# Softmax stage of a four-layer graph network: ScalarE's scaled copies split between its exponentials, two VectorE products back to back, and two of ten numerators on GpSimd

## The chip, the cores and the metric

The kernel runs as one program on one core of a Trainium2 chip. The metric is the device time of that core in microseconds (us), the median of several runs. A core has TensorE (PE in the profile; PEld is its weight load), VectorE (DVE), ScalarE (ACT), GpSimd (POOL) and SyncE (SP, which here only issues transfers). Each engine works through its own list of instructions in order and waits on semaphores, which other engines and transfers raise.

## What is computed

Four graph layers run over 6250 nodes with 16 features and 206250 edges sorted by target node: a double graph convolution, an attention layer with a softmax per edge and channel, a relational layer and an edge-network layer. The change lies in the attention layer (and one semaphore is renamed in the set-up). Cut to what matters, with 256 channels (16 x 16) for each edge:

```python
h_src = feat[src][:, :, None]
e1 = (efeat @ W_msg + b_msg).reshape(E, 16, 16) * h_src      # message
e2 = (efeat @ W_attn + b_attn).reshape(E, 16, 16) * h_src    # logit
seg_max = segment_max(e2, dst)
ex = exp(e2 - seg_max[dst])
denom = segment_sum(ex, dst)
ft = segment_sum(e1 * ex / denom[dst], dst).sum(axis=1)
```

## The kernel before

The edges are laid out as 125 partitions of 1650 edges. The softmax stage goes through them in NB1 = 165 **blocks** of B1 = 10 **steps**; a step is one edge in each partition, with 512 values in each: 256 logits and 256 messages, interleaved in groups of 16. Buffers come in threes (slot s = b % 3). All loops on the chip carry three blocks in a body; what follows is the work for block b, with the name that the text uses. GROUPS = (2, 2, 2) are the steps 0 to 5 (AT = 6), which VectorE multiplies by the gathered features; steps 6 to 9 (NA = 4) are done by ScalarE.

- **Gathers** (GpSimd, `gather`, L594): ten indirect transfers of feature rows, those of steps 6 to 9 first. They wait until ScalarE has done with the slot (`soft_ap`).
- **Edge products**: TensorE multiplies a step's edge features with the weights, into PSUM. `products` (L1094) does two steps at a time for VectorE, `scalable` (L1105) one step for ScalarE, into two banks in turn.
- **Feature products P0, P1, P2** (VectorE, `product`, L1747): two steps each, read from PSUM and multiplied by the gathered features, which is one operand in PSUM and one in the SBUF.
- **Scaled copies C6 to C9** (ScalarE, `scaled`, L808): one of the steps 6 to 9 as 16 small instructions of 32 columns, from PSUM into PB. C7, C8 and C9 of block b+1 and C6 of block b+2 are done while block b is worked on.
- **Maxima T0 to T18** (VectorE, `top`, L1736 and L1740): a running maximum forward over the ten steps and nine steps back. Each depends on the one before.
- **Differences D0 to D5** (TensorE, L1152 and L1153; D5, half as long, L1156 and L1157): logits minus maximum of two steps, with an identity and a negated identity as weights, in two PSUM banks in turn. D0 waits for T10, D1 for T12, D2 for T14, D3 for T16, D4 and D5 for T18. From D2 on, each also waits for the exponential that used its bank two before (`soft_exp`).
- **Exponentials E0 to E5** (ScalarE, L849, E5 at L852): one for each difference.
- **Numerators** (VectorE, `weigh`, L1757): message times exponential, for steps 0-1, 2-3, 4-5 (512 values a partition each) and 6-9 (1024 values), both operands in the SBUF.
- **Carry** (VectorE, L1766) and **first sum** (TensorE, `first_sum`, L1113 and L1115): the block before is joined on; the carry waits for E5 and the second half of the first sum waits for the carry.
- **Row sums R1 to R8** (VectorE, `row_sum`, L1779), the **last sum** (TensorE, `last_sum`, L1121 and L1122, after R8 and E4), and ScalarE's copies of the first and last row (`first_rows` L816, `last_rows` L827, with `last_keep` L820 between).
- **Stores** (SP, L365): maxima and two tables of sums. The second half of a block's sums waits for `last_rows`; P0 of the block three later waits until all of them have landed (`soft_s`).

VectorE's order is written out by hand (`soft` from L1813): while it takes the maxima of block b it does numerators, carry and row sums of block b-1. Before the change it reads: T0, P1, T1, T2, P2, T3, T4, numerators 0-1, T5, carry, T6, T7, R1, T8, numerators 2-3, T9, R2, T10, R3, T11, numerators 4-5, T12, R4, T13, numerators 6-9, T14, R5, T15, R6, T16, P0 of b+1, T17, R7, T18, R8. ScalarE's order in block b is: C7 of b+1, last_rows of b-2, last_keep, C8 of b+1, first_rows of b-1, C9 of b+1, E0, E1, E2, E3, C6 of b+2, E4, E5. TensorE's is: first sum of b-1, edge products of b+1 for C8, C9, P0 and P1, then D0 to D3, the edge products for C6 of b+2 and for P2, D4, D5, the last sum of b-1, the edge product for C7 of b+2.

Of the kernel before, what the change touches and what calls it, by code (L numbers as in the profile page):

```python
# [13 lines left out]
N, E, F = 6250, 206250, 16  # L14
P = 125
# [8 lines left out]
B1 = 10  # L24
NB1 = C // B1
# [3 lines left out]
AT = sum(GROUPS)  # L29
NA = B1 - AT  # L30
SUB = 33
SUBW = C // SUB
MAXES = 2 * B1 - 1
# [74 lines left out]
def graph_layers(nc, A, out):  # L108
# [5 lines left out]
    with ctx:  # L114
# [467 lines left out]
        def _(gp):  # L582
# [57 lines left out]
            narrow("conv2")  # L640

            gp.wait_ge(S("tab_feat"), 16 * (NT + 1))
            for b in range(NB1):
                s = b % 3
                if b >= 3:
                    gp.wait_ge(S("soft_ap"), NA * (b - 2))
                for t in range(AT, B1):
                    gather(GH[:, s, t, :], d_feat, srci[:, b * B1 + t:b * B1 + t + 1], f"soft_late_g{s}")
                for t in range(AT):
                    if b >= 3 and t % 2 == 0:  # L650
                        gp.wait_ge(S("soft_prod"), NG3 * (b - 3) + t // 2 + 1)
                    gather(GH[:, s, t, :], d_feat, srci[:, b * B1 + t:b * B1 + t + 1], f"soft_g{s}")
            for s in range(3):
                gp.wait_ge(S(f"soft_s{s}"), 160 * THIRD)
# [22 lines left out]
        def _(act):  # L677
# [119 lines left out]

            def scaled(b, s, k, t):

                n = t - AT  # L800
                act.wait_ge(S("soft_am"), NA * b + n + 1)
                if n == 0:
                    act.wait_ge(S(f"soft_late_g{s}"), 16 * NA * (k + 1))
                    if not isinstance(b, int) or b >= 3:
                        act.wait_ge(S("soft_num"), 4 * (b - 2))
                bank = (4 + n % 2) * 512
                for i in range(F):
                    ins = act.activation(PB[:, s, n, 2 * F * i:2 * F * (i + 1)], PS[0:P, bank + 2 * F * i:bank + 2 * F * (i + 1)],  # L808
                                         ACT.Copy, scale=GH[:, s, t, i:i + 1])
                ins.then_inc(S("soft_ap"), 1)  # L810

# [17 lines left out]
            def soft(b, s, k, first, left):  # L829
# [12 lines left out]
                for n in range(6):  # L842
                    if n == 4 and left >= 2:
                        scaled(b + 2, (s + 2) % 3, k + (s >= 1), AT)
                    act.wait_ge(S("soft_diff"), 6 * b + n + 1)
                    bank = PS[0:P, (6 + n % 2) * 512:(7 + n % 2) * 512]
                    if n < 5:
                        t = B1 - 2 - 2 * n
                        act.activation(paired(XD[:, s, t:t + 2, :], 0), bank.rearrange("p (x o) -> p x o", o=F), ACT.Exp)\  # L849
                           .then_inc(S("soft_exp"), 1)  # L850
                    else:
                        act.activation(DC, bank[:, 0:CH], ACT.Exp, bias=KR[:, s, 0, 0:1]).then_inc(S("soft_exp"), 1)  # L852

            act.wait_ge(S("h_soft"), 1)
# [52 lines left out]
        def _(pe):  # L907
# [29 lines left out]

            pe.wait_ge(S("diag"), 1)
            pe.matmul(PS[:, 3072:3072 + P], ones[0:P, :], diag[:, :], start=True, stop=True).then_inc(S("run_p"), 1)
# [168 lines left out]
            def first_sum(b, s):  # L1108

                pe.wait_ge(S("soft_exp"), 6 * b + 6)  # L1110
                pe.wait_ge(S("soft_num"), 4 * b + 1)
                bank = PS[0:P, 3584:4096]
# [12 lines left out]
            def soft(b, s, k, first, left):  # L1125
# [9 lines left out]
                for n in range(6):  # L1135
                    if n == 4 and left >= 2:
                        scalable(b + 2, (s + 2) % 3, k + (s >= 1), AT)
# [93 lines left out]
        def _(dve):  # L1231
# [118 lines left out]
            v.tensor_copy(small[0:R, 640:640 + F * F], PS[0:R, 2560:2560 + F * F]).then_inc(S("wrel"), 1)  # L1350
            v.tensor_scalar(diag[:, :], ident[0:P, 0:P], one_run[:, 0:1], None, ALU.mult).then_inc(S("diag"), 1)
            dve.wait_ge(S("run_p"), 1)
# [416 lines left out]
            def row_sum(b, s, t):  # L1769
# [5 lines left out]
                else:  # L1775
                    if t in (2, 4, 6):
                        dve.wait_ge(S("soft_num"), 4 * b + t // 2 + 1)
                    dve.wait_ge(S("soft_sum"), (B1 - 2) * b + t - 1)
# [9 lines left out]
            def late_sums(b, s):  # L1788

                weigh(b, s, 0, 2)  # L1790
                carry(b, s)
# [4 lines left out]
                weigh(b, s, 4, 2)  # L1796
                weigh(b, s, AT, NA)
                for t in range(4, B1 - 1):
# [14 lines left out]
            def soft(b, s, k, left):  # L1813
# [3 lines left out]
                top(b, s, 0)  # L1817
                product(b, s, 1)
                top(b, s, 1)
                top(b, s, 2)  # L1820
                product(b, s, 2)
                top(b, s, 3)
                top(b, s, 4)
                weigh(o, z, 0, 2)
                top(b, s, 5)
                carry(o, z)
                top(b, s, 6)
                top(b, s, 7)
                row_sum(o, z, 1)
                top(b, s, 8)  # L1830
                weigh(o, z, 2, 2)
                top(b, s, 9)
# [7 lines left out]
                top(b, s, 13)  # L1840
                weigh(o, z, AT, NA)
                top(b, s, 14)
                row_sum(o, z, 5)
                top(b, s, 15)
                row_sum(o, z, 6)
                top(b, s, 16)
# [123 lines left out]
```

## Time and profile before

| what | value |
|---|---|
| median of 3 runs | 9713.91 us (9710.63 to 9717.96) |
| the profiled execution's own time | 9719.54 us |
| its span in the trace | 9717.7 us |
| busy in the span: TensorE, VectorE, ScalarE, GpSimd | 80%, 75%, 31%, 71% |
| the softmax stage's first to last carry (L1766) | 3023.6 to 6394.8 us, 164 blocks of 20.56 us |

The stage is a third of the span. In it, VectorE is the busiest engine. The trace's rows give an instruction's start, its duration, the engine, the line in the kernel, the operation, what it writes and reads, the shape, how many instructions are merged in the row, and in square brackets the idle time before it with what ended that time. Durations of neighbours on an engine overlap a little, since the next instruction starts while the last one drains: the cost of an instruction in a full engine is the distance from its start to the next start. The "granted clock" is TensorE's clock as a share of 2.4 GHz; it has two levels, 2.4 and 1.2 GHz (0.5).

### The profile page before, as it was taken

The numbers are of one execution on the slowest core, as the hardware profiler recorded it, in microseconds if no ns is written. First come the engines' busy times: TensorE is split into PE (matmuls) and PEld (weight loads), VectorE is DVE, ScalarE is ACT, GpSimd is POOL, SyncE is SP. The second block draws the span as 40 slices with busy tenths as digits, with TensorE's granted clock in tenths as the row PEclk, the third lists the DMA queues.
The fourth block names the chain that finished last, engine by engine and source line by source line (L and its number), as shares of the span: only waits on it lengthen the run. The fifth ranks groups of instructions, "written<-read, shape, count | busy, mean of one in ns | idle before, by whom it ended". The sixth has DMA issues, their size and how long they took to land.

```text
span 9717.7 us, 129425 instructions
## 1 busy us (share of the span) xinstructions
PE 7811.0 (80%) x35487; PEld 4162.5 (43%) x35487; DVE 7305.6 (75%) x13006; ACT 3031.2 (31%) x12664; POOL 6877.6 (71%) x5177
## 2 busy tenths in 40 slices
PE   0799995999965888888888888845888985899994
PEld 0465553555532333333333333313555653455552
DVE  2566662555536999999999999986888885788884
ACT  0111111000005777777777777731000000000000
POOL 5688886788877766666666666636888886688887
PEclk6899996999987999999999999967999997899996
DMA  1344442233324777777777777765323231433332
GB/s 32 94 114 110 102 104 48 61 76 70 69 38 117 203 203 207 204 203 202 203 205 206 203 202 203 204 192 157 82 70 82 70 82 37 107 100 100 100 105 48
DMA packets 823092, 1218.47 MB, mean 125 GB/s; under 512 B 237316, under 2 KB 687320, under 8 KB 802209
## 3 DMA queue, kind: packets, MB, share of 16 engines
q1 hardware_dynamic: 574895, 999.46, 34.3%
q0 software_dynamic: 212624, 110.62, 9.8%
q10 hardware_dynamic: 35440, 106.85, 3.5%
q8 instruction: 55, 0.90, 0.0%
q14 instruction: 78, 0.64, 0.0%
HBM read 421.45 MB, written 788.86 MB: 125 GB/s over the span
## 4 chain that ended last, share of the span: by engine, by line
POOL 45%; PE 17%; ACT 16%; issue 13%; DVE 5%; DMA 2%; SPq 1%; DVEq 0%; ACTq 0%; POOLq 0%
POOL arena L594 45%; ACT arena L808 14%; PE PS L1152 5%; PE PS L1153 4%; PE PS L1121 2%; PE PS L985 2%; PE PS L1122 1%; ACT arena L849 1%; DVE arena L1912 1%; PE PS L1113 1%; PE PS L1115 1%; PE PS L1105 1%; ACT arena L827 1%; DVE arena L1736 1%; DMA arena<-d_lane 1%
## 5 line engine op out<-in xcount | busy, mean ns | idle before, releaser
L985 PE MATMUL PS<-arena,TB 128*128 128x500 bf16 (+1 forms) x16038 | 3546.8, 376 | 225.0 <-DVE TB L1650 179.3
L594 POOL DMA_INDIRECT arena<-d_feat,srci x1650 | 2127.3, 1289 | 1237.7 <-ACT arena L808 753.8
L985 PEld LDWEIGHTS PS<-arena,TB 128*128 128x128 bf16 x16038 | 1581.0, 100 | 1862.7 <-issue 217.7
L594 POOL DMA_INDIRECT arena<-d_h,srci x1485 | 1959.2, 1319 | 569.8 <-issue 451.1
L808 ACT ACTIVATE arena<-PS,arena 125x32 f32<-125x32 f32 x10560 | 2012.0, 445 | 354.9 <-PE PS L1105 323.8
L1435 DVE TENSOR_SCALAR arena<-arena,lane 128x2000 bf16<-128x2000 f16 (+2 forms) x1848 | 1228.6, 723 | 576.3 <-DMA arena<-d_lane 330.6
L594 POOL DMA_INDIRECT arena<-d_rel,irel x858 | 1208.7, 1409 | 313.0 <-issue 261.2
L594 POOL DMA_INDIRECT arena<-d_nn,srci x759 | 1069.2, 1409 | 295.0 <-issue 230.4
L1152 PE MATMUL PS<-arena,ident 125*125 125x512 f32 x1650 | 962.6, 666 | 312.1 <-DVE arena L1740 211.7
L1447 DVE SCALAR_TENSOR_TENSOR arena<-arena,lane,PS 128x500 f32<-128x500 f16 x891 | 632.2, 712 | 626.0 <-PE PS L988 534.3
L1153 PE MATMUL PS<-arena 125*125 125x512 f32 x1650 | 887.6, 621 | 0.0
L1779 DVE SCALAR_TENSOR_TENSOR arena<-arena 125x512 f32<-125x512 f32 x1155 | 856.7, 742 | 0.3
L1736 DVE SCALAR_TENSOR_TENSOR arena<-arena 125x256 f32<-125x256 f32 x1650 | 786.7, 477 | 31.7
L1467 DVE TENSOR_TENSOR_SCAN arena<-keep,arena 125x50 f32<-125x50 f32 x2640 | 586.0, 296 | 267.7 <-DMA arena<-d_h,srci 258.9
L1008 PEld LDWEIGHTS PS<-fold,arena 128*125 128x125 f32 x5214 | 688.2, 194 | 218.7 <-DVE arena L1447 93.0
L1008 PE MATMUL PS<-fold,arena 128*125 128x16 f32 (+1 forms) x5214 | 639.3, 255 | 120.4 <-ACT arena L718 107.3
L849 ACT ACTIVATE arena<-PS 125x512 f32<-125x512 f32 x825 | 566.5, 754 | 467.6 <-PE PS L1153 467.5
L1740 DVE SCALAR_TENSOR_TENSOR arena<-arena 125x256 f32<-125x256 f32 x1485 | 704.6, 474 | 0.4
L1747 DVE TENSOR_TENSOR arena<-PS,arena 125x1024 f32<-125x1024 f32 x495 | 601.1, 1214 | 39.6 <-DMA arena<-d_feat,srci 33.8
L1152 PEld LDWEIGHTS PS<-arena,ident 125*125 125x125 f32 x1650 | 273.3, 198 | 790.3 <-issue 465.2
L703 ACT ACTIVATE arena<-PS 125x432 f32<-125x432 f32 (+1 forms) x66 | 35.4, 537 | 1672.2 <-PE PS L1008 1672.2
L1757 DVE TENSOR_TENSOR arena<-arena 125x512 f32<-125x512 f32 (+1 forms) x660 | 544.7, 825 | 4.6 <-ACT arena L849 4.6
(285 smaller groups left out, 7692.9 us busy)
## 6 DMA issues: line engine op xcount, KB each, us to landing
d_smax<-arena SPq DMA_DIRECT2D x165, 1120.0 KB
d_sums_low<-arena SPq DMA_DIRECT2D x330, 560.0 KB
d_sums_high<-arena SPq DMA_DIRECT2D x330, 560.0 KB
arena<-d_pick SPq DMA_DIRECT2D x66, 843.8 KB
d_x<-arena ACTq DMA_DIRECT2D x165, 241.7 KB
arena<-d_x SPq DMA_DIRECT2D x165, 241.7 KB
arena<-d_lane SPq DMA_DIRECT2D x66, 527.3 KB
d_rel<-arena SPq DMA_DIRECT2D x50, 669.4 KB
```

The lines of the kernel that those rows point to most:

```text
L594: gp.indirect_dma_start(out=dst, out_offset=None, in_=table, in_offset=bass.IndirectOffsetOnAxis(ap=index, axis=0)).then_inc(S(sem), 16)
L808: ins = act.activation(PB[:, s, n, 2 * F * i:2 * F * (i + 1)], PS[0:P, bank + 2 * F * i:bank + 2 * F * (i + 1)], ACT.Copy, scale=GH[:, s, ...
L849: act.activation(paired(XD[:, s, t:t + 2, :], 0), bank.rearrange("p (x o) -> p x o", o=F), ACT.Exp)\
L985: pe.matmul(PS[:, acc_at(L, q):acc_at(L, q) + w], TB[:, part, g * LANES * F:(g + 1) * LANES * F], OH[L][i][:, g, at:at + w], start=g == 0 ...
L1008: ins = pe.matmul(PS[0:P, 3584 + t * w:3584 + (t + 1) * w], lanes, fold[:, 0:w], start=True, stop=True)
L1152: pe.matmul(bank.rearrange("p (x o) -> p x o", o=F), ident[0:P, 0:P], paired(pairs, 0), start=True, stop=False)
L1153: pe.matmul(bank, neg, XM[:, s, t:t + 2, :].rearrange("p t c -> p (t c)"), start=False, stop=True)\
L1435: ins = v.tensor_scalar(OH[L][i][:, c, 0:n], PI[L][s][:, at:at + n], lane[:, c:c + 1], None, ALU.is_equal)
L1447: v.scalar_tensor_tensor(MK[L][:, acc_slot(L, q), 0:n], LI[L][s][:, q * QW:q * QW + n], lane[:, NG:NG + 1], PS[:, acc_at(L, q):acc_at(L, q ...
L1736: v.scalar_tensor_tensor(wide_row(XM[:, s, n, :]), wide_row(prev), KR[:, s, n, 0:1], logits, ALU.add, ALU.max).then_inc(S("soft_max"), 1)
L1740: v.scalar_tensor_tensor(XM[:, s, t, :], XM[:, s, t + 1, :], KR[:, s, t + 1, 0:1], XM[:, s, t, :], ALU.add, ALU.max).then_inc(S("soft_max" ...
L1779: v.scalar_tensor_tensor(to, last, KR[:, s, t, 1:2], to, ALU.mult, ALU.add).then_inc(S("soft_sum"), 1)
```

## The change

- **ScalarE**: C6 of block b+2 is no longer one run of 16 copies between E3 and E4. Four of its copies follow each of E0, E1, E2 and E3. Its wait for the buffer is now for the numerators 6-7 of block b-1 on VectorE and for GpSimd's multiplication of that block, where it was for all four of VectorE's numerator instructions.
- **TensorE**: the edge product for C6 of block b+2 stands ahead of D0, where it stood ahead of D4. It waits until C8 of block b+1 is done, since it uses the same PSUM bank. The first sum waits for two numerator instructions instead of one.
- **VectorE**: P2 follows P1 directly. The numerator instruction for steps 6 to 9 becomes one for steps 6 and 7, and comes early. The new order is T0, P1, P2, T1, numerators 6-7, T2, T3, numerators 0-1, T4, carry, T5, numerators 2-3, T6, T7, R1, T8, T9, R2, T10, R3, T11, numerators 4-5, T12, R4, T13, R5, T14, R6, T15, T16, P0 of b+1, T17, R7, T18, R8.
- **GpSimd**: the numerators of steps 8 and 9 of block b-4 are one multiplication of 512 values a partition, after the third gather of block b, and it waits until T0 of block b-3 is done. R8 waits for it.
- The semaphore `diag` becomes the fourth count of `wa`; nothing else hangs on that.

```diff
--- before.py
+++ after.py
@@ -639,6 +639,16 @@
             gp.wait_ge(S("tab_conv2"), 16 * (NT + 1))
             narrow("conv2")
 
+            def last_numerators(b):
+
+                s = b % 3
+                gp.wait_ge(S("soft_exp"), 6 * b + 1)
+                if b < NB1 - 1:
+                    gp.wait_ge(S("soft_max"), MAXES * (b + 1) + 1)
+                rows = XD[:, s, B1 - 2:B1, :]
+                gp.tensor_tensor(paired(rows, 1), paired(PB[:, s, NA - 2:NA], 1), paired(rows, 0), ALU.mult)\
+                    .then_inc(S("soft_gp_num"), 1)
+
             gp.wait_ge(S("tab_feat"), 16 * (NT + 1))
             for b in range(NB1):
                 s = b % 3
@@ -646,10 +656,14 @@
                     gp.wait_ge(S("soft_ap"), NA * (b - 2))
                 for t in range(AT, B1):
                     gather(GH[:, s, t, :], d_feat, srci[:, b * B1 + t:b * B1 + t + 1], f"soft_late_g{s}")
+                    if b >= 4 and t == B1 - 2:
+                        last_numerators(b - 4)
                 for t in range(AT):
                     if b >= 3 and t % 2 == 0:
                         gp.wait_ge(S("soft_prod"), NG3 * (b - 3) + t // 2 + 1)
                     gather(GH[:, s, t, :], d_feat, srci[:, b * B1 + t:b * B1 + t + 1], f"soft_g{s}")
+            for b in range(NB1 - 4, NB1):
+                last_numerators(b)
             for s in range(3):
                 gp.wait_ge(S(f"soft_s{s}"), 160 * THIRD)
             for a, table in enumerate((d_smax, *d_sums)):
@@ -795,19 +809,22 @@
             for c, (lo, hi) in enumerate(TAIL):
                 root(f"ln2_{c}", lo, hi)
 
-            def scaled(b, s, k, t):
+            def scaled(b, s, k, t, lo=0, hi=F):
 
                 n = t - AT
-                act.wait_ge(S("soft_am"), NA * b + n + 1)
-                if n == 0:
+                if lo == 0:
+                    act.wait_ge(S("soft_am"), NA * b + n + 1)
+                if n == 0 and lo == 0:
                     act.wait_ge(S(f"soft_late_g{s}"), 16 * NA * (k + 1))
                     if not isinstance(b, int) or b >= 3:
-                        act.wait_ge(S("soft_num"), 4 * (b - 2))
+                        act.wait_ge(S("soft_num"), 4 * (b - 3) + 1)
+                        act.wait_ge(S("soft_gp_num"), b - 2)
                 bank = (4 + n % 2) * 512
-                for i in range(F):
+                for i in range(lo, hi):
                     ins = act.activation(PB[:, s, n, 2 * F * i:2 * F * (i + 1)], PS[0:P, bank + 2 * F * i:bank + 2 * F * (i + 1)],
                                          ACT.Copy, scale=GH[:, s, t, i:i + 1])
-                ins.then_inc(S("soft_ap"), 1)
+                if hi == F:
+                    ins.then_inc(S("soft_ap"), 1)
 
             def first_rows(b, s):
 
@@ -840,8 +857,6 @@
                 if left >= 1:
                     scaled(b + 1, (s + 1) % 3, k + (s == 2), AT + 3)
                 for n in range(6):
-                    if n == 4 and left >= 2:
-                        scaled(b + 2, (s + 2) % 3, k + (s >= 1), AT)
                     act.wait_ge(S("soft_diff"), 6 * b + n + 1)
                     bank = PS[0:P, (6 + n % 2) * 512:(7 + n % 2) * 512]
                     if n < 5:
@@ -1108,7 +1125,7 @@
             def first_sum(b, s):
 
                 pe.wait_ge(S("soft_exp"), 6 * b + 6)
-                pe.wait_ge(S("soft_num"), 4 * b + 1)
+                pe.wait_ge(S("soft_num"), 4 * b + 2)
                 bank = PS[0:P, 3584:4096]
                 pe.matmul(bank, ident[0:P, 0:P], XD[:, s, 0, :], start=True, stop=False)
                 pe.wait_ge(S("soft_carry"), b + 1)
@@ -1133,7 +1150,7 @@
                     products(b + 1, ahead, k1, 1)
 
                 for n in range(6):
-                    if n == 4 and left >= 2:
+                    if n == 0 and left >= 2:
                         scalable(b + 2, (s + 2) % 3, k + (s >= 1), AT)
                     if n == 4 and left >= 1:
                         products(b + 1, ahead, k1, 2)
@@ -1773,8 +1790,10 @@
                     dve.wait_ge(S("soft_first"), b + 1)
                     last = PS[0:P, 3584:4096]
                 else:
-                    if t in (2, 4, 6):
-                        dve.wait_ge(S("soft_num"), 4 * b + t // 2 + 1)
+                    if t in (2, 4):
+                        dve.wait_ge(S("soft_num"), 4 * b + t // 2 + 2)
+                    if t == B1 - 2:
+                        dve.wait_ge(S("soft_gp_num"), b + 1)
                     dve.wait_ge(S("soft_sum"), (B1 - 2) * b + t - 1)
                 v.scalar_tensor_tensor(to, last, KR[:, s, t, 1:2], to, ALU.mult, ALU.add).then_inc(S("soft_sum"), 1)
 
@@ -1787,6 +1806,7 @@
 
             def late_sums(b, s):
 
+                weigh(b, s, AT, NA - 2)
                 weigh(b, s, 0, 2)
                 carry(b, s)
                 row_sum(b, s, 1)
@@ -1816,19 +1835,20 @@
                 dve.wait_ge(S(f"soft_k{s}"), 16 * (k + 1))
                 top(b, s, 0)
                 product(b, s, 1)
+                product(b, s, 2)
                 top(b, s, 1)
+                weigh(o, z, AT, NA - 2)
                 top(b, s, 2)
-                product(b, s, 2)
                 top(b, s, 3)
+                weigh(o, z, 0, 2)
                 top(b, s, 4)
-                weigh(o, z, 0, 2)
+                carry(o, z)
                 top(b, s, 5)
-                carry(o, z)
+                weigh(o, z, 2, 2)
                 top(b, s, 6)
                 top(b, s, 7)
                 row_sum(o, z, 1)
                 top(b, s, 8)
-                weigh(o, z, 2, 2)
                 top(b, s, 9)
                 row_sum(o, z, 2)
                 top(b, s, 10)
@@ -1838,11 +1858,10 @@
                 top(b, s, 12)
                 row_sum(o, z, 4)
                 top(b, s, 13)
-                weigh(o, z, AT, NA)
+                row_sum(o, z, 5)
                 top(b, s, 14)
-                row_sum(o, z, 5)
+                row_sum(o, z, 6)
                 top(b, s, 15)
-                row_sum(o, z, 6)
                 top(b, s, 16)
                 if left >= 1:
                     first_product(b + 1, (s + 1) % 3, k + (s == 2))
```

## Rows read from the trace of the kernel before

**Rows 1.** Busy time by stretches of 1000 us, inside the softmax stage, whole core.

```profile
core 0: us, PE busy (x) PEld busy (x) DVE busy (x) ACT busy (x) POOL busy (x), PEclk, DMA share, GB/s
5000.00:6000.00 1000.00, 840.10 (x2042) 340.47 (x2043) 979.99 (x1704) 768.46 (x3548) 611.05 (x486) 0.96 0.74 204
```

**Rows 2.** Timeline of VectorE over one block (columns: start us, duration us).

```profile
5019.95 0.75 DVE L1779 SCALAR_TENSOR_TENSOR arena<-PS,arena 125x512 f32<-125x512 f32 x1 [0.22 <-PE PS L1115]
5020.61 0.48 DVE L1736 SCALAR_TENSOR_TENSOR arena<-arena 125x256 f32<-125x256 f32 x1
5021.01 0.68 DVE L1757 TENSOR_TENSOR arena<-arena 125x512 f32<-125x512 f32 x1
...
5026.18 1.22 DVE L1757 TENSOR_TENSOR arena<-arena 125x1024 f32<-125x1024 f32 x1
...
5033.08 0.47 DVE L1736 SCALAR_TENSOR_TENSOR arena<-arena 125x256 f32<-125x256 f32 x1
5033.47 1.21 DVE L1747 TENSOR_TENSOR arena<-PS,arena 125x1024 f32<-125x1024 f32 x1
5034.61 0.99 DVE L1736 SCALAR_TENSOR_TENSOR arena<-arena 125x256 f32<-125x256 f32 x2
5035.52 1.22 DVE L1747 TENSOR_TENSOR arena<-PS,arena 125x1024 f32<-125x1024 f32 x1
...
5039.21 1.08 DVE L1736 SCALAR_TENSOR_TENSOR arena<-arena 125x256 f32<-125x256 f32 x2
5040.50 0.75 DVE L1779 SCALAR_TENSOR_TENSOR arena<-PS,arena 125x512 f32<-125x512 f32 x1 [0.22 <-PE PS L1115]
```

**Rows 3.** Timeline of ScalarE over the same block.

```profile
5020.51 0.72 ACT L827 ACTIVATE arena<-PS 125x512 f32<-125x512 f32 x1
...
5021.28 3.08 ACT L808 ACTIVATE arena<-PS,arena 125x32 f32<-125x32 f32 x16
...
5027.18 1.48 ACT L849 ACTIVATE arena<-PS 125x512 f32<-125x512 f32 x2
...
5032.05 0.60 ACT L849 ACTIVATE arena<-PS 125x512 f32<-125x512 f32 x1 [1.21 <-PE PS L1153]
...
5035.25 0.72 ACT L849 ACTIVATE arena<-PS 125x512 f32<-125x512 f32 x1
...
5038.34 2.96 ACT L808 ACTIVATE arena<-PS,arena 125x32 f32<-125x32 f32 x16 [2.00 <-PE PS L1105]
```

**Rows 4.** Timeline of TensorE over the same block: D0, D2, D3, D4, last sum.

```profile
5023.42 1.13 PE L1152 MATMUL PS<-arena,ident 125*125 125x512 f32 x2 [1.32 <-DVE arena L1740]
...
5028.23 1.12 PE L1152 MATMUL PS<-arena,ident 125*125 125x512 f32 x2 [0.95 <-ACT arena L849]
...
5030.05 1.11 PE L1152 MATMUL PS<-arena,ident 125*125 125x512 f32 x2
...
5032.62 1.12 PE L1152 MATMUL PS<-arena,ident 125*125 125x512 f32 x2
...
5036.11 1.12 PE L1121 MATMUL PS<-arena 125*125 125x512 f32 x2 [0.64 <-ACT arena L849]
```

**Rows 5.** Four stretches chosen at the clock's steps; columns as in rows 1.

```profile
5102.67:5106.09 3.42, 1.76 (x6) 0.91 (x7) 3.42 (x8) 3.42 (x20) 2.04 (x2) 1.00 0.46 113
5106.09:5109.50 3.41, 3.41 (x5) 1.34 (x4) 3.41 (x6) 3.41 (x22) 0.00 (x0) 0.50 0.96 263
...
5126.57:5129.98 3.41, 3.41 (x5) 1.32 (x4) 3.41 (x7) 3.41 (x21) 0.00 (x0) 0.50 0.94 252
```

**Rows 6.** Timeline of TensorE in the first of these blocks: D0 and D2.

```profile
5105.62 1.61 PE L1152 MATMUL PS<-arena,ident 125*125 125x512 f32 x2 [1.06 <-DVE arena L1740]
...
5110.86 1.02 PE L1152 MATMUL PS<-arena,ident 125*125 125x512 f32 x2
```

**Rows 7.** Instructions of GpSimd grouped by line, first 200 us of the kernel.

```profile
L588 POOL TENSOR_SCALAR_AFFINE_SELECT ident<-ident 128x128 f32<-128x128 f32 x1 | 0.3, 292 | 0.2 <-POOL ident L586 0.2
```

**Rows 8.** Timeline of GpSimd: first gather of a block.

```profile
5027.98 1.55 POOL L594 DMA_INDIRECT arena<-d_feat,srci  x1 [5.21 <-ACT arena L808]
```

**Rows 9.** VectorE's waits on stores, 3200 to 6300 us (total us, times, longest us).

```profile
DVE arena L1747 <- DMA d_sums_high<-arena: 0.9, 3, 0.4
```

More of the change, by code:

```diff
@@ L852, in soft @@
                         act.activation(DC, bank[:, 0:CH], ACT.Exp, bias=KR[:, s, 0, 0:1]).then_inc(S("soft_exp"), 1)
+                    if n < 4 and left >= 2:
+                        scaled(b + 2, (s + 2) % 3, k + (s >= 1), AT, 4 * n, 4 * n + 4)
             act.wait_ge(S("h_soft"), 1)
@@ L936, in _ @@
                       start=True, stop=True).then_inc(S("wrel_p"), 1)
-            pe.wait_ge(S("diag"), 1)
+            pe.wait_ge(S("wa"), 4)
             pe.matmul(PS[:, 3072:3072 + P], ones[0:P, :], diag[:, :], start=True, stop=True).then_inc(S("run_p"), 1)
@@ L1350, in _ @@
             v.tensor_copy(small[0:R, 640:640 + F * F], PS[0:R, 2560:2560 + F * F]).then_inc(S("wrel"), 1)
-            v.tensor_scalar(diag[:, :], ident[0:P, 0:P], one_run[:, 0:1], None, ALU.mult).then_inc(S("diag"), 1)
+            v.tensor_scalar(diag[:, :], ident[0:P, 0:P], one_run[:, 0:1], None, ALU.mult).then_inc(S("wa"), 1)
             dve.wait_ge(S("run_p"), 1)
@@ L1796, in late_sums @@
                 weigh(b, s, 4, 2)
-                weigh(b, s, AT, NA)
                 for t in range(4, B1 - 1):
```

## The prediction

> **What bounds the kernel now.** The windows view first [rows 1]: VectorE is busy for 980 of 1000 us in the stage, so any gain must shorten its block or leave it waiting. VectorE's timeline of one block comes next [rows 2]. From R1 to R1 it is 5040.50 - 5019.95 = 20.55 us, and the only idle time is 0.22 us ahead of R1, which waits for the second half of the first sum. Beside it runs a second loop, which I read from ScalarE and TensorE together [rows 3, 4]: D2 starts 0.05 us after E0's result, D3 right behind D2, E3 two microseconds after D3 (5030.05 to 5032.05), C6 behind E3, E4 behind C6, the last sum behind E4, C7 2.23 us after the last sum's start (5036.11 to 5038.34), and then C7, last_rows, C8, C9 and E0 in ScalarE's order. No piece of it has slack: two loops of equal length, about 20.55 us, are both tight. Shortening one alone would give nothing. The third thing to read is TensorE's clock. It averages 0.96 here [rows 1]. In some blocks it falls for 3.41 us to 0.50, its lower level of 1.2 GHz, after a stretch in which TensorE was busy for only 1.76 of 3.42 us; the next fall starts 5126.57 - 5106.09 = 20.48 us later [rows 5]. A block with one averages 1 - 0.5 x 3.41 / 20.55 = 0.917, so a mean of 0.96 says that about half of the blocks of this millisecond have one. They lie on D0 and D1: D0 to D2 then takes 5110.86 - 5105.62 = 5.24 us [rows 6], against twice D2 to D3, 2 x 1.82 = 3.64 [rows 4]. These 1.6 us cost nothing now, since D0 normally starts at 5023.42 and E0 only at 5027.18, behind C9 [rows 3, 4].
>
> **VectorE's part.** The instruction of 1024 values (1.22 us) becomes one of 512 (0.68) [rows 2]: -0.54. The idle time ahead of R1 goes: T6 and T7 start at 5039.21 and R1 1.29 us later, where another pair of maxima takes 5035.52 - 5034.61 = 0.91 to the next start (the row gives 0.99 to its end) [rows 2]. That is -0.38. It stays away, because numerators 2-3 now stand between carry and R1 beside the maxima: their 0.6 (5021.01 is followed 0.6 later by the next maximum, as 0.68 less the usual overlap of 0.08) is more than the 0.38 missing. Dependent maxima that stand next to each other cost 0.91 - 2 x 0.40 = 0.11 a pair more (single: 5020.61 to 5021.01), and there are four pairs after (T2-T3, T6-T7, T8-T9, T15-T16) against three: +0.11. Sum: 20.55 - 0.54 - 0.38 + 0.11 = 19.74 us. All else on VectorE keeps its count and its price.
>
> **GpSimd's multiplication.** No row shows a GpSimd instruction with two inputs. The nearest is the 128-column select with one input, 0.29 us [rows 7]. If its time is all fixed cost, the new one takes 0.3; if all of it grows with columns and inputs, 0.292 x 4 x 2 = 2.3. I take 1.2, the middle, since a setup part must be in 0.29. It starts at T0's end or later: the gathers of a block start at 5027.98, three take about 4.9 (one of 1.55, then 1.5 each), so GpSimd arrives at 5032.9, and T0 ends at 5033.55 [rows 2, 8]. P1 and P2 then run for 2 x 1.14 = 2.28 us with one operand in the SBUF each, so the multiplication is over before T1 in my case. Behind it are queued seven gathers, some 10.6 us, whose features are first used over a block later; GpSimd's 5.21 us of idle time a block [rows 8] takes it in. Cost: nothing. If the cover is gone, T1 is late by what hangs over.
> The Trainium skill (SBUF — State Buffer, "Who interferes with whom") says that a VectorE instruction with two SBUF inputs and a GpSimd instruction that reads the SBUF block each other for their whole length. Maxima, numerators and row sums are of that kind, P0 to P2 are not; no row of before can show it. The Trainium skill's GPSIMD Engine Reference ("Elementwise — side-by-side cycle accounting") gives 4497 ns for 2048 values, from which I estimate 1.1 us for 512; by it the sum stays as it is.
>
> **ScalarE's and TensorE's part.** C6 leaves the path between E3 and E4 and goes into ScalarE's waits for TensorE (1.21 us ahead of one exponential [rows 3]; four copies are about 0.7, a quarter of the 16 that start at 5021.28 [rows 3]). Its wait looks only at numerators 6-7 and at GpSimd's multiplication of b-1, both over by T2 of the block, some eight microseconds ahead. The new wait is D0's: it stands behind the edge product for C6, which needs C8 to be over, at 5024.36 [rows 3]. D0 now starts at 5023.42 [rows 4], so this wait will end last. Round the loop, from D4's start: E4 at 2.00, over at 2.60, the last sum at 2.74 (5035.25 + 0.72 to 5036.11), C7 at 4.97, C8 over 5024.36 - (5038.34 - 20.55) = 6.57 later, 11.54; the edge product and D0 at about 11.9 (0.05 to release it, as D2 behind E0, and some 0.3 for the product, an estimate from the gap between D3 and D4); D1, D2 and D3 at 1.72 to 1.82 each; D4 at most 5032.62 - 5030.05 = 2.57 less 0.2 behind D3, since the product for C6 is no longer there. That is 19.2 to 19.7; I use 19.4. By way of E0 (C7 to last_rows 2.72, then 6.67 to E0, 0.6 and 0.05 [rows 3, 4]) D2 is free at 15.0, ahead of 15.4. So with a full clock VectorE would set the block, at 19.74.
>
> **The clock.** D0 to D4 are now one run without slack, right behind TensorE's longest idle stretch. That stretch grows: the edge products are done by about 9.1 in the loop above (they follow C7), D0's product starts at 11.6, against 1.32 us ahead of D0 now [rows 4]. So I expect a fall in nearly every block, and it now costs half of what it covers of the run: 0 when it ends ahead of D0, 1.6 to 1.7 when it lies wholly on the run [rows 6]. The loop is then 19.4 plus 0.5 to 1.7. Falls that repeat come 20.48 us apart [rows 5]. A shorter block meets the next one later in its run, which costs more; a longer block meets it earlier and pays less. Both are drawn to the length of 20.48 us, which the loop reaches with 1.1 us of loss, two thirds of the full price. Anything from 18.8 to 19.9 us for the loop's own length ends there. VectorE, at 19.74, then waits 0.7 us a block, most likely at P0 for the stores: these land late enough even now to hold P0 three times [rows 9], and hang on last_rows, in the slow loop.
>
> **Case A, the forecast.** (20.55 - 20.48) x 163 blocks = 11 us, and some five blocks at the start and end at 19.74, 4 us. From the profiled execution's 9719.5 that gives 9704.5; the median of the runs is 5.6 us lower: 9699 us. Its own range is 9685 to 9712. Chance 0.48.
>
> **Rivals.** B: the clock falls in fewer blocks or beside the run. For it: now it falls in only half of them. Against it: the longer idle stretch. With none, 19.74 binds: 0.81 x 163 = 132 us less, 9582. With half of the blocks paying the full 1.7, the loop has 20.25: 49 us less, 9665. Chance 0.28.
> C, slower: the fall starts only once D0 runs, in every block, and always costs the full 1.7. Then the loop is 19.4 + 1.7 = 21.1, or 0.55 x 163 = 90 us more: 9804. It decides from a mean loss of 20.55 - 19.4 = 1.15. For it: the fall now starts 0.47 us after D0 [rows 5, 6]. Against: its distance of 20.48 does not follow the block of 20.55. Chance 0.12.
> D, the multiplication is long: what it takes beyond 2.2 us holds T1. VectorE has 0.8 us to spare against now, so the kernel gets slower only from 3.0 us, over my upper bound; at 3.5 it is 19.74 + 1.3 = 21.04, 80 us more, 9794. Chance 0.06.
> E, the copies in parts bring nothing: a store that lands late or each change between copy and exponential (0.1 to 0.3) holds the loop at 20.5 to 20.6, 9714. Chance 0.06.
>
> **How the numbers follow.** A measurement tells 0.2%, 19 us, from no change: 9694.5 to 9733.3. A lies within it with 0.40 and below with 0.08, E within, B below: faster 0.36, same 0.46, slower 0.18. The range leaves out the end of B without falls and C and D beyond some 45 us: 9595 to 9760.
>
> **What would show it.** Right: blocks of 20.48 us from carry to carry; a clock near 0.92 over the stage; D0 released by C8's copies; VectorE waiting 0.7 us a block for stores, and no more ahead of R1; GpSimd's multiplication within P1 and P2. Wrong: blocks of 19.7 with VectorE full (B); D0 to D2 always over 5 us with blocks of 21 (C); T1 late behind GpSimd (D); VectorE not waiting at all and yet at 20.5, which would make the 19.74 wrong.

## The result, and the profile after

The changed kernel takes 9789.9 us (9786.4 to 9794.4) against 9715.9 us before: 1.0074 times as long, 95% interval 1.0058 to 1.0090. It was forecast 0.15% faster and is 0.74% slower.

First the windows view of the changed kernel, two stretches inside the stage, to be held against [rows 1].

```profile
core 0: us, PE busy (x) PEld busy (x) DVE busy (x) ACT busy (x) POOL busy (x), PEclk, DMA share, GB/s
4000.00:5000.00 1000.00, 836.40 (x1998) 368.18 (x1997) 942.62 (x1671) 776.97 (x3491) 672.37 (x525) 0.91 0.73 200
5000.00:6000.00 1000.00, 836.66 (x2004) 368.87 (x2003) 942.50 (x1671) 775.87 (x3487) 678.25 (x525) 0.91 0.72 199
```

VectorE is no longer full: 942 of 1000 us where it was 980. The granted clock is 0.91 on average where it was 0.96. The trace's clock records have 164 falls in the stage's 164 blocks, where the kernel before had 56. So practically every block now has a fall of TensorE's clock, and VectorE waits about 1.1 us a block. The same view, cut at the starts of seven carries in a row (the second column is thus the length of a block):

```profile
5067.10:5089.26 22.16, 18.74 (x44) 8.24 (x43) 19.83 (x36) 16.27 (x73) 14.22 (x13) 0.85 0.70 192
5089.26:5110.19 20.93, 17.52 (x44) 7.64 (x43) 19.75 (x36) 16.26 (x73) 14.20 (x11) 0.92 0.73 199
5110.19:5131.15 20.96, 17.55 (x44) 7.64 (x43) 19.79 (x36) 16.26 (x73) 14.31 (x12) 0.92 0.72 200
5131.15:5152.02 20.87, 17.45 (x44) 7.68 (x43) 19.74 (x36) 16.27 (x73) 13.85 (x12) 0.92 0.71 201
5152.02:5172.73 20.71, 17.29 (x44) 7.75 (x43) 19.75 (x36) 16.27 (x73) 14.72 (x12) 0.92 0.73 202
5172.73:5193.33 20.60, 17.18 (x44) 7.61 (x43) 19.75 (x36) 16.27 (x73) 13.56 (x12) 0.92 0.74 203
5193.33:5213.87 20.54, 17.12 (x44) 7.66 (x43) 19.75 (x36) 16.26 (x73) 14.56 (x12) 0.92 0.74 203
sum 146.77, PE 122.86 PEld 54.23 DVE 138.35 ACT 113.86 POOL 99.43; mean PE 17.55 PEld 7.75 DVE 19.76 ACT 16.27 POOL 14.20
```

These seven repeat, with few exceptions, through the whole stage. VectorE's busy time is 19.74 to 19.83 us in each; it was forecast to need 19.74. But the blocks take 20.54 to 22.16 us, 146.77 / 7 = 20.97 on average, against 20.56 before. TensorE's timeline shows where. First an ordinary block (C8's edge product is over, then C6's product, D0, D1, D2; D4 starts at 5041.80), then the long one:

```profile
5032.73 0.69 PE L1122 MATMUL PS<-arena 99*125 99x512 bf16 x1 [2.34 <-ACT arena L824]
5033.21 1.91 PE L1169 MATMUL PS<-arena,ident 125*125 125x512 f32 x2
...
5037.93 1.02 PE L1169 MATMUL PS<-arena,ident 125*125 125x512 f32 x2
```

```profile
5073.87 0.69 PE L1122 MATMUL PS<-arena 99*125 99x512 bf16 x1 [2.34 <-ACT arena L824]
5074.35 1.91 PE L1169 MATMUL PS<-arena,ident 125*125 125x512 f32 x2
...
5077.76 1.91 PE L1169 MATMUL PS<-arena,ident 125*125 125x512 f32 x2
...
5080.64 1.02 PE L1169 MATMUL PS<-arena,ident 125*125 125x512 f32 x2
...
5084.51 1.02 PE L1169 MATMUL PS<-arena,ident 125*125 125x512 f32 x2
```

And the granted clock over the fall of the long block and over that of the ordinary one:

```profile
5073.29:5080.12 6.83, 6.25 (x8) 2.74 (x9) 5.97 (x11) 5.18 (x25) 2.63 (x3) 0.50 0.97 288
5032.33:5035.74 3.41, 3.01 (x4) 1.41 (x5) 3.41 (x8) 3.41 (x19) 0.10 (x1) 0.50 0.91 240
```

TensorE sits idle for 2.34 us until C8 is done, where it waited 1.32 us for T10 before [rows 4]. The clock falls to 1.2 GHz, and the fall lies on D0 to D2. In the ordinary block D0 to D4 takes 5041.80 - 5033.21 = 8.59 us. In the long one the clock stays low for 6.83 us, twice as long, and D0 to D4 takes 5084.51 - 5074.35 = 10.16. What then holds VectorE changes from block to block (the view of who waited for whom, 3200 to 6300 us: total us, times, longest us):

```profile
DVE arena L1764 <- PE PS L1111: 47.1, 66, 1.7
DVE arena L1783 <- PE PS L1139: 46.9, 123, 0.4
DVE arena L1764 <- DMA d_sums_high<-arena: 32.7, 63, 1.6
```

L1764 is P0 to P2, L1783 the carry, L1139 the last sum. The waits for the stores were 0.9 us, three times [rows 9]. None of these is a cause: each is a place where VectorE, ahead by its 1.1 us, meets the slower loop (in the run `fill4` below the falls are gone, and VectorE is full again).

The second loss is at the start of the stage. VectorE, ScalarE and GpSimd at the first blocks (timelines):

```profile
3030.26 0.48 DVE L1757 SCALAR_TENSOR_TENSOR arena<-arena 125x256 f32<-125x256 f32 x1
3040.76 0.75 DVE L1798 SCALAR_TENSOR_TENSOR arena<-arena 125x512 f32<-125x512 f32 x1 [10.02 <-POOL arena L649]
```

```profile
3040.84 0.82 ACT L824 ACTIVATE arena<-PS,arena 125x32 f32<-125x32 f32 x4 [14.75 <-POOL arena L649]
```

```profile
3038.18 1.22 POOL L594 DMA_INDIRECT arena<-d_feat,srci  x1 [0.30 <-issue]
3039.42 1.30 POOL L649 TENSOR_TENSOR arena<-arena 125x512 f32<-125x512 f32 x1
```

R8 of block 0 and C6 of block 3 wait 10 and 15 us for the first multiplication, which has 43 gathers ahead of it in GpSimd's order. From P0's first to its last instruction the stage takes 6446.8 - 2987.7 = 3459.1 us against 3376.9 before, 82 us more: about 20 of them up to the sixth carry, and 0.39 us a block in the other 159. Of these 20, some 15 are idle time of VectorE; the rest comes from four VectorE instructions that take longer beside a late multiplication (see the last experiment). The stages ahead of it took 8 us less in this execution than in the one before; that starting point lies anywhere from 2986 to 2996 us in the runs below, with code that is the same there.

### The profile page after: what moved, and what is told of

Same layout as the page of the kernel before. It is cut to its first block, busy times and chain, and to the rows that moved or that the text cites. A ratio compares the mean times of both kernels' runs of the same rounds, so it can differ in the third digit from the quotient of the medians.

```text
span 9792.6 us, 129916 instructions
## 1 busy us (share of the span) xinstructions
PE 7873.4 (80%) x35487; PEld 4293.5 (44%) x35487; DVE 7247.4 (74%) x13006; ACT 3107.3 (32%) x12664; POOL 7099.7 (73%) x5342
## 4 chain that ended last, share of the span: by engine, by line
POOL 45%; PE 26%; issue 11%; ACT 11%; DVE 4%; DMA 2%; SPq 1%; POOLq 0%; DVEq 0%; ACTq 0%
POOL arena L594 45%; ACT arena L824 10%; PE PS L1169 9%; PE PS L1170 8%; PE PS L1138 2%; PE PS L1002 2%; PE PS L1139 1%; PE PS L1122 1%; ACT arena L844 1%; DVE arena L1931 1%; PE PS L1111 1%; PE PS L1174 1%; PE PS L1173 1%; DMA arena<-d_lane 0%; ACT arena L837 0%
## 5 line engine op out<-in xcount | busy, mean ns | idle before, releaser
L824 ACT ACTIVATE arena<-PS,arena 125x32 f32<-125x32 f32 x10560 | 2072.2, 434 | 313.6 <-PE PS L1122 266.1
L1169 PE MATMUL PS<-arena,ident 125*125 125x512 f32 x1650 | 1022.0, 706 | 19.6 <-ACT arena L864 15.0
L1170 PE MATMUL PS<-arena 125*125 125x512 f32 x1650 | 958.6, 666 | 0.0
L1122 PE MATMUL PS<-arena 99*125 99x512 bf16 x660 | 295.0, 448 | 564.5 <-ACT arena L824 564.5
L1764 DVE TENSOR_TENSOR arena<-PS,arena 125x1024 f32<-125x1024 f32 x495 | 598.4, 1218 | 133.1 <-PE PS L1111 62.5
L864 ACT ACTIVATE arena<-PS 125x512 f32<-125x512 f32 x825 | 494.0, 599 | 470.9 <-PE PS L1170 469.5
L1170 PEld LDWEIGHTS PS<-arena 125*125 125x125 f32 x1650 | 363.0, 220 | 509.4 <-issue 509.4
```

What stands on the lines that cost most here:

```text
L1169: pe.matmul(bank.rearrange("p (x o) -> p x o", o=F), ident[0:P, 0:P], paired(pairs, 0), start=True, stop=False)
L1170: pe.matmul(bank, neg, XM[:, s, t:t + 2, :].rearrange("p t c -> p (t c)"), start=False, stop=True)\
L1764: v.tensor_tensor(XD[:, s, t:t + n, :].rearrange("p t (i c) -> p (t i) c", i=F), PS[0:P, at:at + n * 512].rearrange("p (x c) -> p x c", c= ...
```

## The experiments

**The idle stretch filled.** In `fill4` the two edge products for P1 are issued five times, into the same banks with the same result.

```diff
-            def products(b, s, k, g):
+            def products(b, s, k, g, passes=1):
...
-                for n in range(GROUPS[g]):
+                for n in [*range(GROUPS[g])] * passes:
...
-                    products(b + 1, ahead, k1, 1)
+                    products(b + 1, ahead, k1, 1, 5)
```

> The changed kernel, with the two edge products for P1 issued five times over instead of once (same operands, same banks, same result), so that TensorE works for 1.7 us more in the idle stretch ahead of D0. Theory (the falls of the clock make the block long): no falls, VectorE's 19.7 to 19.8 us sets the block, 1.2 us x 160 = 190 us less than the changed kernel: 9600, ratio to before 0.988. Rival one (D0's new wait for C8 makes the loop of ScalarE and TensorE itself 20.95 long): the added work lies in idle time and changes nothing, 9790. Rival two (GpSimd's multiplication and VectorE block each other): nothing changes either, 9790.

Measured: 9633.4 us, 0.9912 of before (0.9896 to 0.9929), and 33 us over the expected 9600, which left out the late start. The blocks from the sixth on are 19.88 to 19.90 us, those at the very end excepted, and between the fourth and the last block the clock does not fall once:

```profile
5000.00:6000.00 1000.00, 921.77 (x2514) 396.39 (x2515) 984.12 (x1760) 803.26 (x3667) 811.15 (x554) 1.00 0.77 211
```

Adding 1.7 us of useless work to TensorE in each block makes the kernel 157 us faster than the changed one. So the loop of ScalarE and TensorE is shorter than 19.89 us by itself, and the 1.1 us a block are the clock's. Both rivals fall.

**The two halves of the change apart.** In `ve_gp` ScalarE's C6 and its edge product are back where they were; VectorE's and GpSimd's part stays.

```diff
                 for n in range(6):
+                    if n == 4 and left >= 2:
+                        scaled(b + 2, (s + 2) % 3, k + (s >= 1), AT)
...
-                    if n < 4 and left >= 2:
-                        scaled(b + 2, (s + 2) % 3, k + (s >= 1), AT, 4 * n, 4 * n + 4)
...
-                    if n == 0 and left >= 2:
+                    if n == 4 and left >= 2:
                         scalable(b + 2, (s + 2) % 3, k + (s >= 1), AT)
```

> The changed kernel with ScalarE's C6 in one run between E3 and E4 again and its edge product ahead of D4: VectorE's and GpSimd's part alone. Theory: the loop of ScalarE and TensorE is 20.55 as before, D0 has its slack again and the falls cost nothing; blocks of 20.5 to 20.6, and the late start of 13 to 20 us stays: 9727 to 9735. Rival (GpSimd's multiplication makes the block long): blocks of 20.9 and 9790.

`ac_pe` is the reverse: the kernel before, with only these three places as in the changed kernel.

```diff
-                    if n == 4 and left >= 2:
-                        scaled(b + 2, (s + 2) % 3, k + (s >= 1), AT)
...
+                    if n < 4 and left >= 2:
+                        scaled(b + 2, (s + 2) % 3, k + (s >= 1), AT, 4 * n, 4 * n + 4)
...
-                    if n == 4 and left >= 2:
+                    if n == 0 and left >= 2:
                         scalable(b + 2, (s + 2) % 3, k + (s >= 1), AT)
```

> The kernel before with ScalarE's and TensorE's part alone: C6 in parts behind E0 to E3, its edge product ahead of D0; VectorE's order as before, no multiplication on GpSimd. Theory: blocks of 20.9 to 21.0 from the falls of the clock, no late start: 0.4 x 160 = 64 us more than before, 9778. Rival (GpSimd): VectorE's 20.55 sets the block, 9714.

Measured: `ve_gp` 9732.5 us, 1.0015 (1.0005 to 1.0025), and `ac_pe` 9773.1 us, 1.0061 (1.0044 to 1.0078). The same stretch in the two, `ve_gp` first:

```profile
5000.00:6000.00 1000.00, 813.92 (x2035) 347.71 (x2033) 955.20 (x1700) 770.85 (x3551) 691.06 (x533) 0.96 0.74 203
```

```profile
5000.00:6000.00 1000.00, 837.32 (x2002) 368.63 (x2002) 964.97 (x1672) 773.38 (x3488) 671.11 (x477) 0.91 0.72 200
```

With VectorE's part alone the clock is at 0.96 as before; most blocks are 20.52 us long. Blocks with a fall of 3.41 us are mostly 20.5 to 20.7, and the few with one of 6.83 us 22.0. VectorE is idle for 45 of 1000 us: its shorter order is worth nothing while the other loop is 20.5. ScalarE's and TensorE's part alone brings the whole loss of the steady blocks: 0.91, 20.94 us on average, and much the same turns, 20.5 to 22.17, without anything on GpSimd. What the parts of C6 and the moved edge product each do was not run apart.

**The first multiplication.** `start` has the multiplications of blocks 0 to 4 one block of gathers earlier; `b3_only` has all of them so, and nothing else changed.

```diff
-                    if b >= 4 and t == B1 - 2:
-                        last_numerators(b - 4)
+                    if t == B1 - 2 and (3 <= b < 8 or b >= 9):
+                        last_numerators(b - 3 if b < 8 else b - 4)
```

> The changed kernel, with GpSimd's multiplications of blocks 0 to 4 three blocks of gathers behind instead of four; block 5 and on as in the changed kernel. Theory (GpSimd has 43 gathers queued ahead of the first multiplication, and R8 of block 0 and C6 of block 3 wait 10 to 15 us for it once): 13 to 20 us less than the changed kernel, 9770 to 9777, blocks from the eighth on unchanged. Rival (the first blocks are late for the gathers themselves): unchanged, 9790.

```diff
-                    if b >= 4 and t == B1 - 2:
-                        last_numerators(b - 4)
+                    if b >= 3 and t == B1 - 2:
+                        last_numerators(b - 3)
...
-            for b in range(NB1 - 4, NB1):
+            for b in range(NB1 - 3, NB1):
```

> The changed kernel with GpSimd's multiplications one block earlier and nothing else. Theory (the first multiplication's place costs 13 us once, and the falls of the clock cost the rest): 9770 to 9778, blocks of 20.9 to 21.0 on average, in turns of seven. Rival (the place of the multiplication also holds the steady blocks): nearer to 9714.

Measured: `start` 9786.8 us, 1.0067 (1.0051 to 1.0084), 3 us less than the changed kernel, where 13 to 20 were expected. `b3_only` takes 9779.3 us, 1.0065 (1.0048 to 1.0082), 11 us less. Both intervals overlap that of the changed kernel (1.0058 to 1.0090), so the times alone don't show a gain. The traces show one at the start: from P0's first instruction to the sixth carry it is 151 us in the changed kernel, 136 in `start`, 134 in `b3_only` and 131 before. In the whole stage the profile of `start` shows 12.7 us less, and in this execution the stages ahead took 8 us more.

The first block of `start` is 21.4 us long instead of 33.7. But GpSimd is still behind with its gathers in the first blocks of both runs. In `start` the multiplications of blocks 5 to 8, the first that are back at four blocks, come late again, and the eighth block takes 23.5 us. Seven VectorE instructions of `start` are 1.6 to 2.0 us longer beside a late multiplication, 12.5 us in sum, against four and 7.5 us in the changed kernel. The steady blocks of `b3_only`, in turns of seven or eight, average about 20.91 us, 0.05 less: it has 20 falls of 6.83 us where the changed kernel has 24.

**How much work keeps the clock.** In `fill4_b3` both edits stand together; `fill2_b3` and `fill1_b3` have 3 and 2 in place of the 5 passes.

> The changed kernel with the two edge products for P1 issued five times, as in the run fill4, and with each of GpSimd's multiplications one block earlier in its order: that of block b-3 after the third gather of block b. Theory (the first multiplication is late behind 43 gathers, and 33 are early enough; in the steady blocks GpSimd waits for T0 of block b-2 and its gathers still come a block ahead of their use): blocks of 19.9 from the second on, some 15 to 20 us less than fill4's 9633, so 9613 to 9618. Rival (the gathers of the later blocks come late and hold C6 or P0): blocks over 19.9 and more than 9633.

> As fill4_b3 with the two edge products issued three times instead of five, 0.85 us of added work instead of 1.7. Theory (the clock follows TensorE's work in the idle stretch): falls in fewer blocks than in the changed kernel or in none; between 9615 and 9700. If the falls only hang on a wait of some 2 us ahead of D0, they stay away as well, since 1.6 us are left: 9615. Rival (falls come whatever is done): blocks of 20.95 and 9775.

> As fill2_b3 with the two edge products issued twice, 0.43 us of added work. Theory: falls in more blocks than with 0.85 us, in fewer than without, and blocks between 19.9 and 20.95 on average: 9640 to 9740. If the blocks draw to the falls' distance of 20.48 us as forecast for the changed kernel, they stand at 20.48 here: 9705.

| run | added work a block | time, us | against before | steady blocks, us | falls in the stage (of 6.83 us) |
|---|---|---|---|---|---|
| b3_only | 0 | 9779.3 | 1.0065 (1.0048 to 1.0082) | 20.91 | 161 (20) |
| fill1_b3 | 0.43 us | 9789.8 | 1.0072 (1.0056 to 1.0089) | 20.97 | 162 (24) |
| fill2_b3 | 0.85 us | 9619.8 | 0.9895 (0.9879 to 0.9912) | 19.89 | 10 (1) |
| fill4_b3 | 1.7 us | 9621.5 | 0.9893 (0.9877 to 0.9910) | 19.89 | 3 (0) |

`fill4_b3` misses its expected 9613 to 9618 by a few us, since its second to fourth block are still 20.6 to 23.3 us long. There is no slope between: 0.43 us do nothing, against the expected 9640 to 9740, and 0.85 us do all. The clock of `fill2_b3`:

```profile
5000.00:6000.00 1000.00, 879.06 (x2314) 370.65 (x2313) 984.10 (x1761) 804.19 (x3669) 846.50 (x553) 1.00 0.77 211
```

The number of falls itself jumps, from 162 to 10. Why it does so between 0.43 and 0.85 us no run shows. The few falls that are left cost nothing in the steady blocks: those that have one are 19.89 us long like the others. D0 of four blocks in a row, the second with a fall (TensorE's timeline):

```profile
5156.01 1.13 PE L1169 MATMUL PS<-arena,ident 125*125 125x512 f32 x2
...
5175.90 1.85 PE L1169 MATMUL PS<-arena,ident 125*125 125x512 f32 x2
...
5196.80 1.13 PE L1169 MATMUL PS<-arena,ident 125*125 125x512 f32 x2
...
5216.08 1.13 PE L1169 MATMUL PS<-arena,ident 125*125 125x512 f32 x2
```

From D0 to D0 it is 19.89 us, then 20.90 with the fall, then 19.28. The 19.28 are the length of the loop of ScalarE and TensorE when nothing else holds it, and the fall costs 20.90 - 19.28 = 1.62 us. VectorE sets the length, and the other loop makes the single fall up within two or three blocks. In the changed kernel, where nearly each block has a fall, it never can. `fill1_b3` also refutes a block length drawn to 20.48 us: it would have given 9705. The versions of 9620 us take 1.1% less than the kernel before.

**The fall before the change.** `before_fill4` is the kernel before with the same five passes (the diff of `fill4`).

> The kernel before with the two edge products for P1 issued five times. Theory (before, the falls lie in D0's and D1's slack of 1.6 to 1.8 us and cost nothing; both loops are 20.5 without them): no falls, and yet 9700 to 9720. The added 1.7 us starts at about 5022.1 in the block shown and would reach past D0's start at 5023.4, by 0.4 us, which the same slack takes in. Rival (the falls cost something before too): up to 40 us less.

Measured: 9728.1 us, 1.0004 (0.9994 to 1.0013), 8 us over the expected range, but no change against this round's 9725.7 us of the kernel before.

```profile
5000.00:6000.00 1000.00, 889.27 (x2429) 381.10 (x2428) 979.73 (x1700) 765.82 (x3544) 624.32 (x486) 1.00 0.74 204
```

The clock is 1.00, there is no fall in the stage, and the blocks are 20.56 us as before. The falls were there and cost nothing; filling helps only once the loop is tight.

**VectorE beside GpSimd.** `fill4_t8` is `fill4` with the multiplication set beside maxima and row sums instead of P1 and P2.

```diff
-                    gp.wait_ge(S("soft_max"), MAXES * (b + 1) + 1)
+                    gp.wait_ge(S("soft_max"), MAXES * (b + 1) + 9)
```

> The run fill4 with one count changed: GpSimd's multiplication waits until T8 of the block is done, so that it runs beside T9, R2, T10 and R3, which have two operands in the SBUF, and no longer beside P1 and P2. Theory (the Trainium skill's rule in SBUF — State Buffer, Who interferes with whom: such instructions block each other for their whole length): the instruction beside it takes 1.2 to 1.3 us longer in each block, 21.1 instead of 19.9, 200 us more than fill4's 9633. Rival (they only share): below 0.3 us a block, 9633 to 9680.

> The kernel of the run fill4_t8 once more, for its trace: that run's profile fell on an execution in which TensorE's matmuls took about twice their time in the whole kernel, while its four timed runs gave 9798 to 9819. Theory (instructions with two SBUF inputs and GpSimd's multiplication block each other): blocks of 21.0 us, one of T9, R2, T10 or R3 1.1 us longer in each block than in fill4, GpSimd's instruction itself longer or not. Rival (the later gathers hold C6 or P0): VectorE's instructions as long as in fill4, and waits for ScalarE or for a gather.

Measured: 9805.8 us (four executions), 1.0082 (1.0065 to 1.0099), and the second time 9801.9 us, 1.0086 (1.0066 to 1.0106), against `fill4`'s 9633.4. From the second run, VectorE (R1, then T8 and T9, R2) and GpSimd:

```profile
5011.38 0.75 DVE L1798 SCALAR_TENSOR_TENSOR arena<-PS,arena 125x512 f32<-125x512 f32 x1
5012.04 2.20 DVE L1753 SCALAR_TENSOR_TENSOR arena<-arena 125x256 f32<-125x256 f32 x2
5014.16 0.74 DVE L1798 SCALAR_TENSOR_TENSOR arena<-arena 125x512 f32<-125x512 f32 x1
```

```profile
5012.66 1.29 POOL L649 TENSOR_TENSOR arena<-arena 125x512 f32<-125x512 f32 x1 [2.72 <-DVE arena L1753]
```

In its place beside the products the same pair takes 1.08 us (5019.31, from `fill4_b3`), and GpSimd's instruction 1.28:

```profile
5010.87 2.35 DVE L1764 TENSOR_TENSOR arena<-PS,arena 125x1024 f32<-125x1024 f32 x2
...
5019.31 1.08 DVE L1753 SCALAR_TENSOR_TENSOR arena<-arena 125x256 f32<-125x256 f32 x2
```

```profile
5011.11 1.28 POOL L649 TENSOR_TENSOR arena<-arena 125x512 f32<-125x512 f32 x1
```

VectorE loses 1.12 us, GpSimd nothing, and every block is 21.00 us instead of 19.89. The 1.12 us lie on T9 alone. The trace starts T9 at 5012.64 and GpSimd's instruction at 5012.66, so it does not tell which of the two came first. The Trainium skill (SBUF — State Buffer, "Who interferes with whom") says that a VectorE instruction with two SBUF inputs and a GpSimd instruction that reads the SBUF exclude each other, and that a VectorE instruction with at most one SBUF input is not held up. The traces agree: T9 waited, and P1 and P2 take 2.35 us beside the multiplication, as long as without it [rows 2]. The changed kernel pays this price only in the first blocks, where GpSimd comes late. R3 of block 1 takes 2.65 us, although it starts 0.8 us before the multiplication does (3056.83):

```profile
3056.03 2.65 DVE L1798 SCALAR_TENSOR_TENSOR arena<-arena 125x512 f32<-125x512 f32 x1
```

That is 1.91 us more than usual, and more than the multiplication's whole 1.30. Four VectorE instructions of the first blocks are longer by 1.7 to 2.0 us, 7.5 us in sum. Why they lose more than the multiplication's own length stays open.

## Why the prediction was wrong, point by point

- **Two tight loops of 20.55 us.** Right: shortening VectorE's alone leaves 20.52 (`ve_gp`). Shortening the other alone did not give nothing, as the text has it, but cost 0.38 us a block through the falls (`ac_pe`).
- **VectorE's sum, 19.74 us.** Nearly: 19.89. The pairs T6-T7 and T8-T9 have 1.00 us to the next start each, not 0.91. So the idle time that goes was 0.29 and not 0.38, and the fourth pair costs 0.20 and not 0.11. Together 0.18 us, 0.15 of which show.
- **GpSimd's multiplication.** 1.28 us where 1.2 was taken from a span of 0.3 to 2.3, and within P1 and P2 in the steady blocks. Rival D, a multiplication too long for P1 and P2, did not occur. Beside T9 the same 1.28 us cost 1.1 a block (`fill4_t8`).
- **"Cost: nothing" for GpSimd** was a wrong step. It was read from the steady blocks alone, where GpSimd has 5.21 us idle. At the start of the stage it has none: 43 gathers stand ahead. Up to the sixth carry the stage runs some 20 us behind: VectorE is idle for 15 us more, and late multiplications lengthen its instructions by 7.5. An earlier place saves 15 to 17 us up to there in the traces (`start`, `b3_only`), of which the times, with their noise, show 3 to 11. The text counted 4 us of gain in these blocks.
- **The new wait of D0 for C8, and a loop of 19.4 us.** Right. TensorE waits 2.34 us there, and the loop by itself takes 19.28 us (`fill2_b3`). A block with a single fall wholly on the run takes 20.93, that is 19.28 and 1.65 for the fall.
- **A fall in nearly every block.** Right: 164 falls in 164 blocks, 0.91 over the stage. The text's "about half of the blocks" for the kernel before holds for the millisecond that it looked at; over the stage it was a third, 56 falls.
- **Blocks drawn to 20.48 us.** This is the step that failed. The approach is there: 20.93, 20.96, 20.87, 20.71, 20.60, 20.54, each block meeting its fall earlier than the one before. It does not stay there. Close to 20.5 the clock remains low for 6.83 us, D0 to D4 takes 10.16 us, and the 22.16 us of this block throw the next fall back behind D0. The price of a fall was capped at 1.7 us in the text. All falls of the steady blocks before were of 3.41 us (55, and a single one of 6.83 us at 6379.26 in the last block), so the rows gave no reason to expect more; here one in seven costs 22.17 - 19.28 = 2.9. The mean is 20.97, 0.49 over the forecast, 76 us over 157 blocks. With the 24 us at the start, less some 8 us by which the stages ahead were shorter in this execution, that is the distance from 9699 to 9790.
- **VectorE waits at P0 for the stores.** Only in part: 32.7 us from 3200 to 6300 us, 0.2 a block out of 1.1.
- **The rivals.** C named the sign and nearly the size, 9804, with the fall always at its full price of 1.7. That its price fits the measured mean, 20.97 - 19.28 = 1.69, is luck: the mean is made of falls at 1.3 to 1.7 us in most blocks and at 2.9 in one of seven. Its own mechanism, a fall that follows D0 at a fixed distance, is not what happens: in the changed kernel the fall starts anywhere from 1.1 us before D0 to 0.8 us after it. A chance of 0.12 was too little for "the clock costs more than 1.15 us on average", since the range of its price, 0.5 to 1.7, reached well over that point.

What stays open is why the clock remains low for twice the time in one block of seven. It starts nearly where it did in the block before (6.19 us after the carry against 6.25). The rows of the first 3.41 us of the two falls, the long one second, differ little, and most of the difference is idle time of TensorE ahead of C6's edge product:

```profile
5052.78:5056.19 3.41, 2.86 (x4) 1.36 (x5) 3.41 (x8) 3.41 (x20) 1.75 (x1) 0.50 0.99 262
5073.26:5076.67 3.41, 2.80 (x4) 1.40 (x5) 3.41 (x8) 3.41 (x21) 0.30 (x1) 0.50 0.93 233
```

No run changed that alone. The long fall is not bound to the closed loop: `ve_gp`, whose D0 has its slack back, has seven of them, and most come after a row of short ones.

## What to carry to other kernels

A wait that moves onto TensorE ahead of its longest run of matmuls cost twice here: its own length, and the clock that fell during it and stayed low in the run. So before a loop is closed over TensorE, look where the falls lie now, and count their full price into the loop if the slack under them goes. If the idle stretch can't be avoided, repeat a harmless matmul in it. For an instruction that is appended to a queue, read the start of the stage as well as its steady part, and set a two-input GpSimd instruction beside VectorE instructions that read from PSUM.

## What was not expected of the hardware

- 0.85 us of repeated matmuls a block took 160 us off a kernel of 9779 us, and 0.43 us took nothing.
- GpSimd's multiplication of 512 values in 125 partitions took 1.28 to 1.30 us both beside VectorE work with one SBUF input and beside work with two; the waiting was VectorE's, 1.12 us in the steady blocks of `fill4_t8` and up to 2.0 us in the first blocks of the changed kernel. Only the changed kernel's last multiplication took longer itself, 2.18 us.
- In its first execution `fill4_t8` took 15929 us, in four others 9798 to 9819. TensorE was busy for 94% of the span, its matmuls took up to 1.7 times as long as in `t8_again` (mean of L1169 1.12 us against 0.64), and no other engine's instructions were more than 2% longer. The figures for `fill4_t8` above are those of the other four.
